# The first FFN's weights loaded and split inside its own stage, half of the loads issued by ACT

## The reference

```python
x = L0_attn_x                                   # 8 x 256 x 128, float32
x = x + 0.5 * _L0_ffn_ref(_layernorm(x, axis=-1), ...)
x = x + _L0_attn_ref(_layernorm(x, axis=-1), ...)          # RWKV
x = x + 0.5 * _L0_ffn_ref(_layernorm(x, axis=-1), ...)
x = x + 0.5 * _L1_ffn_ref(_layernorm(x, axis=-1), ...)
x = x + _L1_attn_ref(_layernorm(x, axis=-1), ...)          # Mamba 2
x = x + 0.5 * _L1_ffn_ref(_layernorm(x, axis=-1), ...)
```

## Time and profile before

| | us |
|---|---|
| median of 3 timed runs | 785.05 (782.3 to 785.35) |
| the profiled execution | 779.87 |
| its span | 778.2 |
| PE busy | 686.9 (88% of the span) |
| DVE busy | 568.3 (73%) |
| ACT busy | 414.7 (53%) |
| POOL busy | 323.1 (42%) |
| SP's last issue in `setup()` | 7.11, for 1.20 |
| POOL's last constant in `setup()` | 1.22, for 0.29 |

### The profile page before, as it was taken

One profiled execution on the slowest core, in us unless ns is written; L12 is line 12 of the kernel. 1 busy time (PEld: TensorE's weight loads), 2 busy tenths in 40 slices (PEclk: granted clock), 3 DMA queues, 4 the chain that ended last, 5 costly groups with the idle time before them and its releaser, 6 DMA issues. The chain is left out here.

```text
span 778.2 us, 12435 instructions
## 1 busy us (share of the span) xinstructions
PE 686.9 (88%) x4044; PEld 511.1 (66%) x4044; DVE 568.3 (73%) x1289; ACT 414.7 (53%) x747; POOL 323.1 (42%) x404
## 2 busy tenths in 40 slices
PE   0889995668789999999999697999999994999997
PEld 0667774234356777777778586677777773677785
DVE  3688866889978788888988636456565575689775
ACT  2456585857415555556655336455555551555553
POOL 1357784020316566555666416122212201357354
PEclk9999998879999999999999769899999996999999
DMA  5245530000003322212223000000000000223132
GB/s 155 82 151 150 181 110 0 1 0 0 1 0 111 109 94 86 91 60 81 83 81 84 1 1 1 1 3 1 0 0 0 0 2 0 85 80 103 61 96 68
DMA packets 32757, 43.10 MB, mean 55 GB/s; under 512 B 5184, under 2 KB 15424, under 8 KB 32704
## 3 DMA queue, kind: packets, MB, share of 16 engines
q1 hardware_dynamic: 32704, 42.46, 17.7%
HBM read 41.13 MB, written 1.31 MB: 55 GB/s over the span
## 5 line engine op out<-in xcount | busy, mean ns | idle before, releaser
L558 POOL TENSOR_TENSOR p_prod<-p_p,p_gate_row 128x512 f32<-128x512 f32 x128 | 200.1, 1572 | 126.3 <-DVE p_p L417 68.4
L320 ACT ACTIVATE p_sil<-p_ps_a 128x512 f32<-128x512 f32 x176 | 105.1, 597 | 132.7 <-PE p_ps_a L100 126.9
L422 DVE TENSOR_TENSOR p_hlo<-p_prod,p_hhi 128x512 fp32r<-128x512 f32 x176 | 150.5, 856 | 3.0 <-ACT p_hhi L329 2.7
L417 DVE TENSOR_TENSOR p_p<-p_sil,p_ps_b 128x512 f32<-128x512 f32 x128 | 87.3, 682 | 58.6 <-ACT p_sil L320 47.2
L329 ACT CAST p_hhi<-p_prod 128x512 fp32r<-128x512 f32 x176 | 108.0, 614 | 24.1 <-POOL p_prod L558 24.1
L98 PE MATMUL p_ps_acc<-p_hhi,w_downhi 128*128 128x512 f32 x176 | 71.9, 409 | 3.0 <-DVE p_hlo L422 2.9
L98 PE MATMUL p_ps_a<-xt_hi,w_uphi 128*128 128x512 f32 x176 | 74.5, 423 | 0.0
L98 PE MATMUL p_ps_b<-xt_hi,w_uphi 128*128 128x512 f32 x176 | 71.3, 405 | 0.4 <-DVE p_prod L417 0.4
L100 PE MATMUL p_ps_a<-xt_hi,w_uplo 128*128 128x512 f32 x176 | 70.3, 399 | 0.0
L99 PE MATMUL p_ps_a<-xt_lo,w_uphi 128*128 128x512 f32 x176 | 70.2, 399 | 0.0
L100 PE MATMUL p_ps_b<-xt_hi,w_uplo 128*128 128x512 f32 x176 | 70.2, 399 | 0.0
(11 more groups left out here) (300 smaller groups left out, 1436.5 us busy)
## 6 DMA issues: line engine op xcount, KB each, us to landing
p_gate_row<-gate_rows SPq DMA_DIRECT2D x128, 256.0 KB, 3.3
w_rawbuf<-in_L_ffn_fc_w_dram SPq DMA_DIRECT2D x3, 512.0 KB, 5.6
w_rawbuf<-in_L_ffn_w_dram SPq DMA_DIRECT2D x3, 512.0 KB, 6.5
out_dram<-x SPq DMA_DIRECT2D x4, 256.0 KB, 3.6
w_rawbuf<-in_L_ffn_shared_w_dram SPq DMA_DIRECT2D x3, 256.0 KB, 6.3
mb_xraw<-in_L_attn_W_B_dram SPq DMA_DIRECT2D x1, 512.0 KB, 4.4
mb_xraw<-in_L_attn_W_C_dram SPq DMA_DIRECT2D x1, 512.0 KB, 5.0
gate_rows<-p_gates_t SPq DMA_DIRECT2D x16, 16.0 KB, 1.4
```

What stands on the lines that cost most here:

```text
L320: nc.scalar.activation(sil[:, u % 2], ps_a[:, u % 2], ACT.Silu).then_inc(c["sil"].sem, 1)
L417: nc.vector.tensor_tensor(dst, sil[:, u % 2], ps_b[:, u % 2], ALU.mult).then_inc(c["p1"].sem, 1)
L422: nc.vector.tensor_tensor(hlo[:, u % R], prod[:, u % R], hhi[:, u % R].bitcast(F32), ALU.subtract).then_inc(c["hlo"].sem, 1)
L558: G.tensor_tensor(prod[:, u % R], p1[:, u % 2], gate_row[:, e % ROWS], ALU.mult).then_inc(c["prod"].sem, 1)
```

## The change

`setup()` and its barrier are gone. `ffn_stream` gets `opening=(w0_set, x_dram)`, and the first stage itself does the following.

- The raw pieces of the first FFN land in the raw buffers of the second FFN (`places`), in the order gate and up, router, experts 0 to 3, down, experts 4 to 7, the experts' down weights (splits 0 to 5). SP waits for the low part of split 5 before it issues the second FFN's first loads.
- ACT issues gate, up, router and down on its own queue, ahead of its first copy. SP issues x in three parts (block 0, block 1, blocks 2 and 3) with the three large pieces in between.
- The splits stand at written places between the first operations of block 0, on ACT and on DVE. `measure(1)` and `measure(2)` on DVE and `scale(2)` on POOL move to later places, each behind a wait for its part of x.
- PE waits for the low parts that it needs: two before `route(0)`, three before unit 2, five before unit 6, four before `down(0, 0)`, six before `down(0, 2)`.
- POOL fills the constants at the head of the stage; PE and DVE wait for them (`filled`).
- The router bias is loaded with the RWKV vectors.

```diff
@@ tensor
+            def split_up_to(k):
+                if opening:
+                    pe.wait_ge(c["raw_lo"].sem, c["raw_lo"].at(k))
...
+                if n == 0 and u in (2, 6):
+                    split_up_to(3 if u == 2 else 5)
...
+                if n == 0 and u in (0, 2):
+                    split_up_to(4 if u == 0 else 6)
...
+            if opening:
+                pe.wait_ge(c["filled"].sem, c["filled"].at(4))
             if not begun:
                 turn_x(0)
+            split_up_to(2)
             route(0)
@@ scalar
+            if opening:
+                opening[0].load(act, slice(0, 2))
+                opening[0].load(act, slice(3, 4))
+            for k in range(3):
+                own(k)
             if not begun:
                 high_x(0)
+            own(3)
             take_logits(0)
             gate(0, 0)
             tanh(0)
             gate(0, 1)
+            own(4)
             gate(0, 2)
+            own(5)
             take_gates(0)
@@ vector
             if not begun:
+                landed(0)
                 measure(0)
+                own(0)
+                own(1)
                 normal(0)
-                measure(1)
+                own(2)
+                if not opening:
+                    measure(1)
                 low_x(0)
+                if opening:
+                    landed(1)
+                    measure(1)
+            own(3)
             normal(1)
-            measure(2)
+            if not opening:
+                measure(2)
             choose(0)
             for u in range(3):
                 gated(0, u)
+            if opening:
+                landed(2)
+                measure(2)
             low(0, 0)
             low_x(1)
+            own(4)
             gated(0, 3)
             low(0, 1)
+            own(5)
@@ gpsimd
-            scale(2)
+            if not opening:
+                scale(2)
             weights(0)
+            if opening:
+                scale(2)
@@ sync
                     if between and e == ROWS:
+                        if opening:
+                            sp.wait_ge(c["raw_lo"].sem, c["raw_lo"].at(OWN))
                         between(sp)
...
+                take(0, slice(0, BT))
+                own.load(sp, slice(2, 3))
+                take(1, slice(BT, 2 * BT))
+                own.load(sp, slice(4, None))
+                take(2, slice(2 * BT, TILES))
@@ program
+        S = w0.shared
+        raw = w1_set.raws
+        places = [raw[0][:, 0:S], raw[2], raw[3], raw[1][:, 0:S], raw[4], raw[5]]
+        w0_set = RawWeights(None, counts, "w0", [w0_jobs[k] for k in (0, 2, 3, 1, 4, 5)], one_semaphore=False, raws=places)
...
-        setup()
```

More of the change, by code:

```diff
@@ L108, in __init__, with ffn_stream @@
         self.units, self.shared = weights.units, weights.shared
-def ffn_stream(nc, tag, counts, spare, sb, ps, x, xt, consts, kinds, gate_dram, norm, loads=(), splits=(), out_dram=None, entry=None, begun=False, heads=False):
+def ffn_stream(nc, tag, counts, spare, sb, ps, x, xt, consts, kinds, gate_dram, norm, loads=(), splits=(), out_dram=None, entry=None, begun=False, heads=False, opening=None):
     splits = split_jobs(splits)
+    OWN = len(opening[0].jobs) if opening else 0
     LEAD, BEHIND = 4, 2
@@ L128, in ffn_stream @@
     HEADED = BLOCKS + 2 if heads else BLOCKS
+    POOL_SPLITS, DVE_SPLITS = [{at: tuple(OWN + k for k in some) for at, some in t.items()} for t in (POOL_SPLITS, DVE_SPLITS)]
     SPLITS = {**POOL_SPLITS, **DVE_SPLITS}
@@ L386, in next_rows, with own @@
                     last.then_inc(c["r_tok"].sem, 1)
+            def own(k):
+                if opening:
+                    split_hi(nc, act, c, splits[k])
+            if opening:
[3 more added lines that the diff above has]
+                own(k)
             if not begun:
                 high_x(0)
+            own(3)
             take_logits(0)
@@ L527, in next_stage, with own, landed @@
                     prepare_mixing(nc, dve, c, entry["vec"], consts, entry, entry["weights"])
+            def own(k):
+                if opening:
+                    split_lo(nc, dve, c, splits[k], k)
+            def landed(k):
+                if opening:
+                    dve.wait_ge(c[f"x{k}"].sem, c[f"x{k}"].at(16))
+            if opening:
+                dve.wait_ge(c["filled"].sem, c["filled"].at(4))
             if not begun:
+                landed(0)
                 measure(0)
+                own(0)
+                own(1)
                 normal(0)
-                measure(1)
+                own(2)
+                if not opening:
+                    measure(1)
                 low_x(0)
+                if opening:
+                    landed(1)
+                    measure(1)
+            own(3)
             normal(1)
-            measure(2)
+            if not opening:
+                measure(2)
             choose(0)
@@ L636, in store, with take @@
                 sp.dma_start(out_dram[:, some], x[:, some]).then_inc(c["io"].sem, 16)
+            if opening:
+                own, source = opening
+                def take(k, some):
+                    sp.dma_start(x[:, some], source[:, some]).then_inc(c[f"x{k}"].sem, 16)
+                take(0, slice(0, BT))
[3 more added lines that the diff above has]
+                take(2, slice(2 * BT, TILES))
             for n in range(BLOCKS):
@@ L665, in ffn_stream @@
         c["io"].base += 16 * NBLK
+    if opening:
+        c["filled"].base += 4
     c["raw_hi"].base += len(splits)
@@ L2048, in program @@
         names = ("a b sil p1 hhi hlo prod row0 row1 row2 row3 store stored down route xn xt xhi xlo lg lgs lgt gth gates gt gts acc_s ot out "
-                 "stats moments veps rstd score gap key top hot share g12 filled io raw0 raw1 raw2 raw3 raw4 raw5 raw_hi raw_lo rw_raw w1_raw mb_raw").split()
+                 "stats moments veps rstd score gap key top hot share g12 filled io raw0 raw1 raw2 raw3 raw4 raw5 raw_hi raw_lo x0 x1 x2 rw_raw w1_raw mb_raw").split()
         counts = {n: Count(sem("s_" + n)) for n in names}
@@ L2133, in program @@
             vectors.append((rw["tmrow"][:, q], a["L0_attn_" + n].rearrange("q r p -> q (r p)").broadcast_to([P, P])))
+        vectors.append((bias[:], a["L1_ffn_expert_bias"].rearrange("(a e) -> a e", a=1).broadcast_to([P, EXPERTS])))
         rw_set = RawWeights(None, counts, "rw", [
@@ L2140, in program @@
         w1_set = RawWeights(owned(raw_scope), counts, "w1", w1_jobs, one_semaphore=False)
[L2142 to L2181, removed]
@@ L2219, in program @@
                            loads=(lambda sp: w1_set.load(sp, slice(0, 4)), load_rest, mb.load) if k == 0 else (),
-                           splits=(w1_set,) if k == 0 else (mb,) if later == "mamba" else (), heads=later == "mamba", entry=entry if k == 0 else None, begun=k > 0 and STAGES[k - 1] == "rwkv",
+                           opening=(w0_set, x_dram) if k == 0 else None,
+                           splits=(w0_set, w1_set) if k == 0 else (mb,) if later == "mamba" else (), heads=later == "mamba", entry=entry if k == 0 else None, begun=k > 0 and STAGES[k - 1] == "rwkv",
                            out_dram=out_dram if k + len(stages) == len(STAGES) else None)
```

20 lines of the change are left out of this document (16 added, 4 removed).

## The result

The changed kernel takes 776.28 us, median of four runs (773.64 to 777.04), against 785.2 for the kernel before (782.3 to 785.67): ratio 0.9888, 95% interval 0.9853 to 0.9923, so 8.9 us less. Two later series of the same two kernels, with more runs, gave 0.9906 (0.9881 to 0.9930) and 0.9919 (0.9891 to 0.9947), 7.4 and 6.3 us. The forecast was 776.0 us, 9.1 less.

The account below looks back on a forecast made before the run. PE was taken to bound the first FFN from 50 us on, so head savings reach the end: 10.5 gained minus 1.4 for row 4 is 9.1, and 785.05 - 9.1 = 776.0 us; range 773.0 to 782.0 for eight in ten.

Parts of the forecast that it names:

- The head: Start of the first FFN: block 0 no longer waits for all transfers and splits; 10.5 us gained.
- R: Mark in the head where xlo of block 0 is complete; forecast to move from 22.47 to 12.0 us.
- lower bound of 4.7: Earliest landing of x's first quarter, if it goes first; 5.4 us was forecast, 7.2 the upper bound.
- DVE idles there for 1.55 us, hidden: Splits 0 and 1 on DVE fit its wait for rstd before block 0's normalisation; 0.9 us if cover were gone.
- the even share: SP's and ACT's queues share the DMA engines evenly, so x's first quarter lands at 5.4 us.
- The second queue: Issuing half of the weights from ACT is worth next to nothing by itself.
- ACT's inserted copies: Splits 4 and 5 on ACT delay block 0's copy of the gates, and PE behind it, by 1.2 us.
- SP's hold: SP's second-FFN loads wait for split 5's low part: issued 14.7 us after R instead of 10.9, 3.8 late.
- row 4 is 1.4 late: Block 0's gate row 4, queued behind the held loads, lands 1.4 us late, since bytes set the landing.
- PE's own delay: PE's 1.2 us delay from ACT's splits lies inside row 4's 1.4, as both end in the same wait.
- rival (a): Row 4 is 3.8 us late, PE idles 4.6 at block 1's gates, clock drops; 779.9 or 782.9 us; chance 0.20.
- the third: Sign of being wrong: PE's gap at block 1's gates above 4 us with 1.2 GHz matmuls behind it.

Follow-up runs that it names:

- e1: The kernel before, unchanged, run and profiled a second time: 782.99 us, ratio 1.0005.
- e8: The changed kernel, unchanged, run and profiled again: 776.79 us, ratio 0.9906 to the kernel before.
- e5: The changed kernel with all loads on SP's queue and none issued by ACT: 775.95 us, ratio 0.9892 to the kernel before.
- e6: The kernel before with gate, up, down and router issued by ACT, nothing else changed: 782.2 us, ratio 0.9992.
- e3: The changed kernel with SP waiting for four low parts instead of six before the second FFN's first loads: 774.6 us, ratio 0.9889 to the kernel before.
- e10: The kernel before with SP also waiting for POOL's first product before issuing the second FFN's first loads: 785.98 us, ratio 1.0047.
- e11: The changed kernel, unchanged, a third time, on the same chip as e12: 776.02 us, ratio 0.9919 to the kernel before.
- e4: The kernel before with the second FFN's first loads issued behind gate row 7 of block 0: 781.3 us, ratio 0.9981.
- e2: The changed kernel with the second FFN's first loads issued behind gate row 7 of block 0: 774.0 us, ratio 0.9885 to the kernel before.
- e12: The same edit to the changed kernel as e2, repeated on the same chip as e11: 774.56 us, ratio 0.9900 to the kernel before.
- e7: The changed kernel with block 0's normalisation, xlo and xhi put ahead of weight splits on DVE and ACT: 777.21 us, ratio 0.9909 to the kernel before.

## Why the prediction was right, and where it was not

**The head.** Forecast 10.5 us at R, measured 9.9 (10.3 between e1 and e8). Two errors nearly cancel. The landing of x's first part was taken at 5.4 and came at 3.9, below the lower bound of 4.7. And "DVE idles there for 1.55 us, hidden" failed: the work of splits 0 and 1 would have fitted, but their operands had not landed. The step priced two DVE operations and never asked when up and the router, second and third in ACT's queue, arrive; it cost 2.2 us (6.6 to 8.9). With the even share that I took, ACT's first three pieces should have been there by 5.4; gate was (3.4 us from its issue), up and the router were not. The Trainium skill, DMA: Bandwidth & Descriptors, "Queues, rings and completion order", has each DMA engine go round robin between its rings packet by packet, which for packets of one size would give the even share. The trace doesn't agree: the landings of the last two were later than that (5.2 and 6.3 us from issue), and in e5 the same two pieces, in SP's queue behind x, landed 2.8 and 2.4 us from theirs.

**The second queue.** Worth nothing, as forecast (e6), and in this order of work a loss inside the head: R is 1.4 us earlier without it (e5), too little for the timed runs to show.

**ACT's inserted copies.** Forecast 1.2 us later at the copy of the gates. Measured from R 8.98 against 7.34: 1.6 (1.4 in e8). Of this 0.5 is not ACT: the turned logits came 4.03 behind R (16.57) instead of 3.53, as PE's matmuls were still at the lower level there.

**SP's hold.** The loads went out 14.85 us behind R; forecast 14.7. The next term is the one that was mis-sized: "row 4 is 1.4 late". POOL's product with it started 24.4 behind R, not 22.2: 3.6 late in this profile, 2.9 and 3.0 in the two others. I had the row that gave it (6.9 us from row 4's issue to its landing, which makes 3.8), and set it aside for a count of bytes. That count took 0.34 MB per us; from 29 us, 1.6 behind the issue, to 35 us the changed kernel moved 1.57 MB, 0.26 per us, and POOL started 1.9 us after that. e3, e8, e10 and e11 show 9.2 to 10.3 us from the issue of the loads to POOL's start, however empty the queue was. Nor was PE's own delay inside the other, as the forecast had it: from R to block 1's gates it is 23.8 us before and 23.6 in e4, 25.1 and 25.0 in e2 and e12, where nobody waits for row 4, and 27.0 to 27.6 in the three profiles of the changed kernel. Some 1.4 us are what ACT and DVE were given, and the hold adds 1.8 to 2.6 to them. So rival (a), to which I gave 0.20, is what happened: gap 3.15 to 3.54, the lower clock behind it for some 3 us. Of the signs of being wrong none showed as it was written, but the third did by half: the lower clock came with a gap under 4 us. In the store-to-store column all seven executions with a gap of 2.94 or more take 32.1 to 33.7 us, all seven with 1.99 or less take 30.2 to 31.0. Its price for the clock, 1.5 to 4.5 us, was measured at 1.5 to 3.

**Why the number still held.** By the first profile, the sum with these terms is 9.9 - 3.6 - 0.2 = 6.1 at block 1's gates (46.25 to 40.11), and 3.8 at the start of the RWKV stage, behind the clock. That is less than rival (a)'s 5.2, by 1.4. But the kernel before doesn't always run as in that profile. In e1 it had a gap of 2.94 and lost its clock too. Against e1, e8 gains 10.3 us at R, 8.5 at block 1's gates, 7.9 at the RWKV stage and 7.0 in span. The timed ratios, 6.3 to 8.9 us, lie near this pair. So the reference of my sum was a short execution, by up to 4.3 us at the end of the stage, and my loss at row 4 was too small by 1.5 to 2.2 with another 1.5 to 3 of clock behind it: the two make up for each other. The sign, the place and the size of the gain were right for the reason given (x no longer waits for the weights); 776.0 being met to 0.3 us was in part luck. The two later series, at 7.4 and 6.3 us, put the gain lower than the 9.1 of the sum.

How often the kernel before runs with the lower clock there can't be told from three profiles of its order (one of three). The first profile of the changed kernel had another peculiarity: from the first gate store behind the RWKV stage to the first one behind the Mamba stage it took 430.8 us where ten others took 433.0 to 433.8 and three 434.2 to 434.6. Its span of 773.8 was short by some 2 us for that reason. The change touches nothing there; why it varies is open.

**What stays open.** Moving the loads behind row 7 brings the end of the stage forward by 3.7 to 4.1 us in traces and shortens the timed runs by some 2.3. Where the rest goes isn't settled. The stretch from the start of the RWKV stage to the next FFN's first gate store ranged over 106.3 to 108.4 us from trace to trace, which is enough to hide it, but in no order that I can name.

## What to carry to other kernels

A step is hidden only if its operands are there: for each operation put into an idle slot, ask what it waits for and when that lands, not only how long it takes. When a transfer that somebody waits for stands behind larger ones, take the measured time from issue to use in the same order of issues before any count of bytes. And before a sum is set against one profile, take a second profile of the same kernel: here one kernel showed a gap of 1.99 us with the full clock in one profile and of 2.94 us with the lower one in the other, and the spans differ by 4.6 us.

## What the runs showed of the hardware

A gap of 1.99 us on a full PE left the granted clock at 2.4 GHz (also 1.95, 1.60 and four times 1.42); gaps of 2.94 to 5.12 us came with the 1.2 GHz level in all seven cases, and the stretch to the next store was 1.5 to 3 us longer. No profile has a gap between 1.99 and 2.94 here. By stretches of 1 us the granted clock stayed at the lower level for 3.4 us in the changed kernel's three profiles and e7, and for 6.8 us in e1, e5 and e10. It fell 0.7 to 1.3 us after PE had gone on in the changed kernel's first profile, e8 and e7, and while PE stood still in the other four.

A load of 4 KB issued on ACT's queue third, while SP's queue held 0.5 MB pieces, took 5.3 to 6.3 us to land (7 profiles); on SP's queue behind 0.5 MB it took 2.4 (e5). x's first 256 KB landed 3.0 us after their issue.

A gate row of 256 KB queued behind 1.3 MB of loads was in use 9.2 to 11.0 us after the first of these loads was issued, over ten profiles; a row alone landed 3.2 us after its own issue.
